# Row sums of the attention: seven tiles added on GpSimd for one pass, and one division for text and image

## The reference, cut to what matters

```python
img_x = attention(q, k_img, v_img)
txt_x = attention(q, k, v, kv_mask)      # kv_mask: only the first context_lens[b] text keys
out = (txt_x + img_x).reshape(b, -1, DIM)
```

## Time and profile before

| | us |
|---|---|
| median of three runs | 3730.16 (3720.81 to 3733.33) |
| the profiled execution | 3734.04 |
| its span on the core | 3731.9 |
| `attend` in the profile, first scores to last exp | about 910 to 2758 |

### The profile page before, as it was taken

One profiled execution on the slowest core, in us unless ns is written; L12 is line 12 of the kernel. 1 busy time (PEld: TensorE's weight loads), 2 busy tenths in 40 slices (PEclk: granted clock), 3 DMA queues, 4 the chain that ended last, 5 costly groups with the idle time before them and its releaser, 6 DMA issues. The chain is left out here.

```text
span 3731.9 us, 54675 instructions
## 1 busy us (share of the span) xinstructions
PE 3280.9 (88%) x18048; PEld 1744.2 (47%) x18048; DVE 2313.9 (62%) x3780; ACT 1483.5 (40%) x2101; POOL 15.6 (0%) x34
## 2 busy tenths in 40 slices
PE   6999999994999999999999999999966631899993
PEld 5788787772333333333333333333224421777772
DVE  5666676654566667667666676676626659333335
ACT  3344444331555555555555555555431110122222
POOL 0000000000000000000000000000000000000000
PEclk8999999995999999999999999999887775999996
DMA  5666666678253453543534535435214550201005
GB/s 153 169 165 165 165 166 166 166 137 151 58 120 78 101 111 69 119 98 81 119 82 97 116 69 113 101 78 119 49 34 158 164 205 3 71 23 45 25 21 180
DMA packets 405977, 402.04 MB, mean 108 GB/s; under 512 B 43569, under 2 KB 326257, under 8 KB 403321
## 3 DMA queue, kind: packets, MB, share of 16 engines
q1 hardware_dynamic: 363272, 367.44, 41.8%
q10 hardware_dynamic: 42624, 33.56, 2.7%
HBM read 262.98 MB, written 137.92 MB: 107 GB/s over the span
## 5 line engine op out<-in xcount | busy, mean ns | idle before, releaser
L834 ACT ACTIVATE at_probs<-at_st 128x1024 f32<-128x1024 f32 (+1 forms) x832 | 852.0, 1024 | 866.1 <-PE at_st L713 860.6
L862 DVE TENSOR_REDUCE at_cm<-at_mx 128x2 f32<-128x896 f32 x768 | 822.0, 1089 | 450.0 <-PE at_mx L729 450.0
L713 PE MATMUL at_st<-at_qst,at_kst 101*128 101x512 f32 (+1 forms) x1664 | 612.2, 449 | 19.2 <-ACT at_probs L834 18.8
L713 PEld LDWEIGHTS at_st<-at_qst,at_kst 101*128 101x128 f32 (+1 forms) x1664 | 243.7, 186 | 731.0 <-ACT at_probs L834 655.4
L752 PE MATMUL at_acc<-at_probs,at_vt 128*32 128x512 f32 (+2 forms) x3584 | 480.1, 610 | 21.8 <-ACT at_ev L815 21.6
L764 PE MATMUL at_acc<-at_probs,at_ones 128*32 128x512 f32 (+2 forms) x3584 | 479.8, 610 | 0.0
L729 PE MATMUL at_mx<-at_kmx,at_qmx 33*128 33x448 f32 (+1 forms) x2048 | 380.1, 423 | 43.5 <-DMA at_kmx<-stack_rows 33.5
L729 PEld LDWEIGHTS at_mx<-at_kmx,at_qmx 33*128 33x128 f32 x2048 | 170.5, 189 | 296.1 <-issue 240.9
L862 DVE TENSOR_REDUCE at_top<-at_mx 128x2 f32<-128x514 f32 x256 | 176.8, 691 | 122.2 <-PE at_mx L729 117.1
L1274 ACT ACTIVATE ff_h<-ff_psa,ff_b1c,alpha 128x512 f32<-128x512 f32 x128 | 99.6, 779 | 378.1 <-PE ff_psa L1256 378.1
L879 DVE RECIPROCAL at_rl<-at_ev 128x512 f32<-128x512 f32 x64 | 210.1, 3324 | 49.4 <-ACT at_ev L815 49.4
(11 more groups left out here) (182 smaller groups left out, 4027.7 us busy)
## 6 DMA issues: line engine op xcount, KB each, us to landing
at_kst<-k_high SPq DMA_DIRECT2D x256, 200.1 KB
at_kmx<-k_high SPq DMA_DIRECT2D x64, 400.2 KB
at_kst<-k_low SPq DMA_DIRECT2D x128, 200.1 KB
pj_xin<-in_ctx_dram SPq DMA_DIRECT2D x96, 256.0 KB, 4.2
k_high<-pj_kh SPq DMA_DIRECT2D x96, 256.0 KB, 3.2
k_low<-pj_kl SPq DMA_DIRECT2D x96, 256.0 KB, 4.7
values<-pj_vs SPq DMA_DIRECT2D x96, 256.0 KB, 4.6
at_vt<-values SPq DMA_DIRECT2D x32, 768.0 KB
```

Source lines behind the costliest of these rows:

```text
L713: pe.matmul(st[0:kn, h % 2, :], kst[p][:, h, t * P:t * P + kn], qst[p][:, h, :], start=True, stop=True).then_inc(S["st_done"], 1)
L834: act.activation(probs[0:kn, SLOT[t], 2 * run:2 * run + 2, :], st[0:kn, :, :], ACT.Exp, scale=SCALE).then_inc(S["exp_done"], 2)
L862: dve.tensor_reduce(dst, mx[:, 2 * slot:2 * slot + 2, 0:kn], AX.X, ALU.max).then_inc(S["mx_free"], 1)
```

## The change

- Sums: the text tiles 0, 1, 2, 4, 5, 7 and 8 have no sums pass of their own. GpSimd adds their probabilities (128x2048 f32 each) in six additions into a new tile `added`, and one pass over `added` stands for all seven. It runs at (12, 1). The passes left are 8 (`SUMMED`): tiles 3, 6, 9 and the text half of 10 at (4, 1), (7, 1), (10, 1), (11, 1); `added` at (12, 1); and the three image passes, all at (0, 1) of the next group.
- Division: GpSimd's `join` forms VT·SI, VI·ST, ST·SI and the sum of the first two (four operations of 128x512); VectorE's `finish` is one reciprocal of ST·SI, one operation that brings in the bias, and one product.
- Waits: a slot of `probs` that held one of the seven tiles is free when its values pass and its addition are done (two waits in `ring` for one). ScalarE copies ST behind (12, 1) and no longer behind (12, 0). The copy of VT waits for `join` in place of `finish`.

```diff
+    SUMMED = [(3, 0, P), (6, 0, P), (9, 0, P), (10, 0, HALF), (None, 0, P), (11, 0, P), (10, HALF, P), (12, 0, KLAST)]
+    NSUM, SUM_IMG0 = len(SUMMED), 5
+    SUMS_AT = {4: [0], 7: [1], 10: [2], 11: [3], 12: [4]}
+    ADDED = [1, 2, 4, 5, 7, 8]
+    NADD = len(ADDED)
@@ GpSimd
+            def join(G, p):
+                pool.wait_ge(S["v_free"], 2 * G + 2)
+                pool.wait_ge(S["s_free"], 2 * G + 2)
+                if not known(G, 1):
+                    pool.wait_ge(S["res_done"], G)
+                pool.tensor_tensor(part[:, 0, :], ev[p][:, VT, :], ev[p][:, SI, :], ALU.mult).then_inc(S["joined"], 1)
+                pool.tensor_tensor(part[:, 1, :], ev[p][:, VI, :], ev[p][:, ST, :], ALU.mult).then_inc(S["joined"], 1)
+                pool.tensor_tensor(rl[:, 0, :], ev[p][:, ST, :], ev[p][:, SI, :], ALU.mult).then_inc(S["joined"], 1)
+                pool.wait_ge(S["joined"], 4 * G + 2)
+                pool.tensor_tensor(rl[:, 1, :], part[:, 0, :], part[:, 1, :], ALU.add).then_inc(S["joined"], 1)
+
+            def add(G, n):
+                t = ADDED[n]
+                pool.wait_ge(S["exp_done"], NST * G + HG * (t + 1))
+                if n:
+                    pool.wait_ge(S["add_done"], NADD * G + n)
+                elif not known(G, 1):
+                    pool.wait_ge(S["s_done"], NSUM * (G - 1) + SUM_IMG0)
+                so_far = added[:] if n else probs[:, SLOT[0]]
+                pool.tensor_tensor(added[:], so_far, probs[:, SLOT[t]], ALU.add).then_inc(S["add_done"], 1)
+
+            def body(i, par):
+                G = 2 * i + par
+                if not known(G, 1):
+                    join(G - 1, 1 - par)
+                for n in range(NADD):
+                    add(G, n)
@@ TensorE, sums and body
+                if t is None:
+                    pe.wait_ge(S["add_done"], NADD * (G + 1))
                 for h in range(HG):
                     cols = slice(h * HD, (h + 1) * HD)
-                    done = pe.matmul(acc[cols, 1, :], ones[r0:r1, :], probs[r0:r1, SLOT[t], h, :],
-                                     start=q in (0, IMG0), stop=q in (IMG0 - 1, NPASS - 1))
+                    src = added[:, h, :] if t is None else probs[r0:r1, SLOT[t], h, :]
+                    done = pe.matmul(acc[cols, 1, :], ones[r0:r1, :], src,
+                                     start=q in (0, SUM_IMG0), stop=q in (SUM_IMG0 - 1, NSUM - 1))
...
-                            for q in (12, 13):
-                                if run == 0:
+                            if run == 0:
+                                for q in (12, 13):
                                     values(G - 1, *before, q)
-                                else:
+                            else:
+                                for q in range(SUM_IMG0, NSUM):
                                     sums(G - 1, q)
                         elif t > 0 and run == 0:
                             values(G, i, par, t - 1)
                         elif t > 0:
-                            sums(G, t - 1)
+                            for q in SUMS_AT.get(t, []):
+                                sums(G, q)
@@ ScalarE, ring and body
+                if u == 0 or u in ADDED:
+                    act.wait_ge(S["v_done"], NPASS * G + u + 1)
+                    act.wait_ge(S["add_done"], NADD * G + max(ADDED.index(max(u, 1)), 0) + 1)
+                else:
+                    act.wait_ge(S["s_done"], NSUM * G + max(q for q in range(NSUM) if SUMMED[q][0] == u) + 1)
...
-                        if (t, run) == (12, 0):
-                            evacuate(G, par, ST, 1, "s_done", "s_free")
+                        if (t, run) == (12, 1):
+                            evacuate(G, par, ST)
@@ VectorE, finish
-                for k, s in enumerate((ST, SI)):
-                    dve.reciprocal(rl[:, k, :], ev[p][:, s, :]).then_inc(S["fin"], 1)
-                for k, v in enumerate((VT, VI)):
-                    dve.wait_ge(S["fin"], 4 * G + k + 1)
-                    dve.tensor_tensor(part[:, k, :], ev[p][:, v, :], rl[:, k, :], ALU.mult).then_inc(S["fin"], 1)
-                dve.wait_ge(S["fin"], 4 * G + 4)
+                dve.wait_ge(S["joined"], 4 * G + 4)
+                dve.reciprocal(part[:, 1, :], rl[:, 0, :]).then_inc(S["fin"], 1)
+                dve.scalar_tensor_tensor(part[:, 0, :], rl[:, 0, :], bv[:, bass.ds(G, 1)], rl[:, 1, :], ALU.mult, ALU.add).then_inc(S["fin"], 1)
+                dve.wait_ge(S["fin"], 2 * G + 2)
                 if not known(G, 2):
                     dve.wait_ge(saved[p], 16 * i)
-                dve.scalar_tensor_tensor(res[p][:], part[:, 0, :], bv[:, bass.ds(G, 1)], part[:, 1, :], ALU.add, ALU.add).then_inc(S["res_done"], 1)
+                dve.tensor_tensor(res[p][:], part[:, 0, :], part[:, 1, :], ALU.mult).then_inc(S["res_done"], 1)
```

More of the change, by code:

```diff
@@ L570, in attend @@
     IMG0 = 11
+    SUMMED = [(3, 0, P), (6, 0, P), (9, 0, P), (10, 0, HALF), (None, 0, P), (11, 0, P), (10, HALF, P), (12, 0, KLAST)]
[3 more added lines that the diff above has]
+    NADD = len(ADDED)
     RING = 4
     SLOT = [3, 0, 1, 2, 0, 1, 2, 0, 1, 2, 0, 1, 2]
-    LAST_PASS = [max(q for q in range(NPASS) if PASS[q][0] == t) for t in range(KT)]
     VT, ST, VI, SI = range(4)
@@ L582, in attend @@
         probs = a.sb("probs", [P, RING, HG, SQ])
+        added = a.sb("added", [P, HG, SQ])
         ones = a.sb("ones", [P, HD])
@@ L600, in attend @@
         names = ("const_set bv_set st_done exp_done v_done s_done mx_full mx_free neg_step top_full top_copied "
-                 "v_free s_free fin res_done const_dve").split()
+                 "v_free s_free add_done joined fin res_done const_dve").split()
         S = {n: a.sem(n) for n in names}
@@ L699, in _ @@
                 pool.memset(where.bitcast(F32), value).then_inc(S["const_set"], 1)
+            def join(G, p):
[23 more added lines that the diff above has]
+                    add(G, n)
+            pairs(pool, body)
+            join(GROUPS - 1, 1)
         @block.tensor
@@ L756, in sums @@
             def sums(G, q):
-                t, r0, r1 = PASS[q]
+                t, r0, r1 = SUMMED[q]
                 if q == 0 and not known(G, 1):
                     pe.wait_ge(S["s_free"], 2 * G)
-                if q == IMG0:
+                if q == SUM_IMG0:
                     pe.wait_ge(S["s_free"], 2 * G + 1)
+                if t is None:
+                    pe.wait_ge(S["add_done"], NADD * (G + 1))
                 for h in range(HG):
                     cols = slice(h * HD, (h + 1) * HD)
-                    done = pe.matmul(acc[cols, 1, :], ones[r0:r1, :], probs[r0:r1, SLOT[t], h, :],
-                                     start=q in (0, IMG0), stop=q in (IMG0 - 1, NPASS - 1))
+                    src = added[:, h, :] if t is None else probs[r0:r1, SLOT[t], h, :]
+                    done = pe.matmul(acc[cols, 1, :], ones[r0:r1, :], src,
+                                     start=q in (0, SUM_IMG0), stop=q in (SUM_IMG0 - 1, NSUM - 1))
                 done.then_inc(S["s_done"], 1)
@@ L809, in copy_top, with evacuate @@
                                ACT.Copy).then_inc(S["top_copied"], 1)
-            def evacuate(G, p, kind, bank, done, free):
-                act.wait_ge(S[done], NPASS * G + (IMG0 if kind < VI else NPASS))
+            def evacuate(G, p, kind):
+                if kind in (VT, VI):
+                    act.wait_ge(S["v_done"], NPASS * G + (IMG0 if kind == VT else NPASS))
+                else:
+                    act.wait_ge(S["s_done"], NSUM * G + (SUM_IMG0 if kind == ST else NSUM))
                 if kind == VT and not known(G, 2):
-                    act.wait_ge(S["res_done"], G - 1)
+                    act.wait_ge(S["joined"], 4 * (G - 1))
+                bank, free = (0, "v_free") if kind in (VT, VI) else (1, "s_free")
                 act.activation(ev[p][:, kind, :], acc[:, bank, :], ACT.Copy).then_inc(S[free], 1)
             def ring(G, t):
[L818 to L823, removed]
+                if t < 4:
+                    if known(G, 1):
+                        return
+                    G = G - 1
+                u = max(u for u in range(t if t >= 4 else KT) if SLOT[u] == SLOT[t])
+                if u == 0 or u in ADDED:
+                    act.wait_ge(S["v_done"], NPASS * G + u + 1)
+                    act.wait_ge(S["add_done"], NADD * G + max(ADDED.index(max(u, 1)), 0) + 1)
+                else:
+                    act.wait_ge(S["s_done"], NSUM * G + max(q for q in range(NSUM) if SUMMED[q][0] == u) + 1)
             def body(i, par):
@@ L838, in body @@
                             if (t, run) == (0, 1):
-                                evacuate(G - 1, 1 - par, VI, 0, "v_done", "v_free")
+                                evacuate(G - 1, 1 - par, VI)
                             if (t, run) == (1, 0):
-                                evacuate(G - 1, 1 - par, SI, 1, "s_done", "s_free")
```

(11 more changed lines are left out.)

2 lines of the change are left out of this document (removed).

## The result

The changed kernel takes 3950.48 us (median of four runs, 3930.48 to 3954.05). The kernel before takes 3731.74 beside it (3720.81 to 3733.98). The ratio is 1.058, with a 95% interval of 1.054 to 1.062. The profiled execution of after is 3954.05, its span 3951.9: 220.0 more than the 3731.9 of before.

What follows compares the result with a forecast made beforehand. TensorE bounds the kernel, with the scores-exp loop of 1.90 us right under it. Nearly balanced groups, gains in groups 0 and 30 and a longer end sum to −2.6 us: 3728 us, eight in ten within 3714 to 3775.

Steps and rivals of the forecast that it cites:

- The loop of 1.90: In `attend`, scores, exp and hand-over make 0.82 + 1.02 + 0.06 = 1.90 us, which no work taken from TensorE can shorten.
- The third pass at (0, 1): The image pass moved to step (0, 1), bound by TensorE, was to cost its full 1.0 us a group.
- The wait at (11, 0): One more ScalarE wait in `ring`, counted only at (11, 0), where TensorE waits for ScalarE's copy: 0.07 us.
- The group: A group of `attend`, 57.27 us before, was to change by −1.04 + 1.00 + 0.07 = +0.03 us at full clock.
- VectorE's `finish`: Division cut to one reciprocal, one product and one addition, nobody waiting soon: 0, except in the last group.
- an addition: GpSimd's sum of two 128x2048 tiles was put at 4.8 us, just in time for the exps: forecast 0.
- rival A: GpSimd late: additions over 4.8 us delay the exp; 3773 at 5.3 us, 3850 at 6.1; chance 0.18 with mild B.
- B: GpSimd and VectorE block each other: up to +1700 us; mild forms share 0.18, strong form shares 0.03 with new stalls.
- The end of `attend`: After the last group, one more pass, then `join`, one reciprocal and one product: +1.4 us.
- rival C: TensorE's idle time lowers its clock: +500 us (4230) if every group drops, +10 to +20 for single drops; chance 0.08.
- Groups 0 and 30: Groups partly at half clock: −3.7 us for group 0, −2.2 for group 30 if its 1.82 us gap comes again.
- D: The 1.82 us gap behind ScalarE's first-run code goes, 3718, or comes twice, 3738; it cost about 10 us; chance 0.11.

## Why the prediction was wrong, point by point

**What held.** The loop of 1.90, named the second bound: at full clock an empty step lasts 1.90 in after and in the four experiments that have any. The third pass at (0, 1): 3.05 became 4.05, its full 1.0. The wait at (11, 0): the forecast 0.07 shows as 2.42 for 2.37 at (12, 0), 0.05. The group: 57.33 where the clock holds, forecast 57.30. VectorE's `finish`: three operations, nobody late.

GpSimd: an addition takes 4.55 us, forecast 4.8; the estimate from the Trainium skill (GPSIMD Engine Reference, Performance versus the Vector engine), 4497 ns, is within 1.3% of the measured 4554. The operations of `join` take 1.27, as forecast. Here is the group that the prediction followed, in a group with the clock at 1.00 up to these steps; (1, 0) starts at 1501.7:

```profile
1504.27 1.27 POOL L711 TENSOR_TENSOR at_part<-at_ev 128x512 f32<-128x512 f32 x1 [26.90 <-ACT at_ev L861]
...
1509.20 4.56 POOL L725 TENSOR_TENSOR at_added<-at_probs 128x2048 f32<-128x2048 f32 x1
...
1513.84 13.85 POOL L725 TENSOR_TENSOR at_added<-at_added,at_probs 128x2048 f32<-128x2048 f32 x3
...
1515.04 1.02 ACT L884 ACTIVATE at_probs<-at_st 128x1024 f32<-128x1024 f32 x1 [1.03 <-PE at_st L749]
```

`join` starts 2.5 behind (1, 0) (forecast 2.7), addition 0 is done at 1513.8, and the exp of (4, 0) at 1515.04, 13.3 behind (1, 0) as forecast, had waited for TensorE's scores and not for `added`. So rival A didn't come. B neither: reductions and additions ran side by side. The rule of the Trainium skill on a port shared as a lock (SBUF — State Buffer, "SBUF: two separate sides") left the reductions out, and the window with 720 us of additions agrees. In this group `finish` begins at 1542.58, 2.6 us behind the last addition.

The end of `attend`: `join`, reciprocal, bias, product.

```profile
2980.99 1.26 POOL L711 TENSOR_TENSOR at_part<-at_ev 128x512 f32<-128x512 f32 x1 [16.19 <-issue]
...
2984.65 1.26 POOL L715 TENSOR_TENSOR at_rl<-at_part 128x512 f32<-128x512 f32 x1
...
2985.94 3.35 DVE L927 RECIPROCAL at_part<-at_rl 128x512 f32<-128x512 f32 x1 [44.10 <-POOL at_rl L715]
...
2989.90 0.69 DVE L932 TENSOR_TENSOR at_res<-at_part 128x512 f32<-128x512 f32 x1
```

The stretch grew by 2.3, forecast 1.4. The terms that the sum has were right to 0.2, but it leaves one out: `finish` also has the operation that brings in the bias, 0.65 us, between the reciprocal and the product.

**The step that failed** is the weighing of rival C, the clock. The sum has a group at +0.03 us "but for the clock below"; in the loop it came to +6.4 us a group (177.9 in 28), nearly all of it steps at the half clock. The prediction said itself that "the other 0.8 us of each pass becomes idle time of TensorE", that the clock had fallen behind a gap of 1.82 and not in the last group with 0.18 idle a step, and "My gaps lie between". Then it gave C 0.08, with the argument that TensorE is at work 80% of the time. Neither ground holds. The known points bracketed the new gap and said nothing on its side; between ends so far apart 0.08 was no reading but a wish. And the busy share is a mean: in the experiment with one pass out only one step of 26 had less work on TensorE than before, and the clock fell in every ninth group.

The last group shows both sizes of rest. In before nearly every one of its steps has a rest of 0.16 to 0.18, and it kept the clock. In after its seven empty steps have no maxima either, so TensorE rests for 1.17 us in them, and the clock fell twice: scores take 1.22 in (2, 1) and (3, 0), and again in (6, 1) to (7, 1). Here are (2, 0), behind the first such rest, and (2, 1):

```profile
2928.21 0.73 PE L749 MATMUL at_st<-at_qst,at_kst 101*128 101x512 f32 x2 [1.17 <-ACT at_probs L884]
2928.88 1.52 PE L788 MATMUL at_acc<-at_probs,at_vt 128*32 128x512 f32 x8
2930.33 1.22 PE L749 MATMUL at_st<-at_qst,at_kst 101*128 101x512 f32 x2
```

The group took 55.3 for 48.9, 5.4 more than forecast. In before and in the four experiments without an empty step the last group has no step at the half clock. So the row of 0.18 was read rightly; it said nothing on rests four to seven times as long.

**The price of C** was worked out for a fall in every group that lasts until tile 10: "2.3 more than now together" for a tile, 16 us a group and +500 in all. Its steps were right: 3.90 to 4.06 in run 0 (forecast 3.9) and 2.40 when empty (forecast 2.42). The longest falls of the loop, from (4, 0) to (10, 1), cost 17.2 us. What was too large is how often and how long: of the 22 groups that fell, six did so behind (3, 1), six behind (5, 1) and ten only behind (8, 1) or (9, 1), and six had no fall. That gives 178 us in 28 groups, and 220 in all. The prediction had nothing between "One or two single drops" (+10 to +20) and +500.

**Small terms.** The sum says groups 1 to 30 and counts 29, which is right, as group 30 has a term of its own. Groups 0 and 30 were forecast at −3.7 and −2.2 and gave −1.9 and +16.1. Group 0 had one more fall, behind (9, 1), which cost it about 1.4. Group 30 began with a stall in its first step, which lasted 6.79, where before had its stall of 1.82 in tile 8:

```profile
2838.03 1.02 ACT L884 ACTIVATE at_probs<-at_st 128x1024 f32<-128x1024 f32 x1 [5.22 <-issue]
...
2839.20 1.19 PE L749 MATMUL at_st<-at_qst,at_kst 101*128 101x512 f32 x2 [3.50 <-ACT at_probs L884]
```

The next step, 7.38, is the one with three passes, now at the half clock, and the clock stayed down through (8, 1) and fell once more behind (9, 1). That is what D's "As well it may come twice" was about, but D had put 10 us on it, and the group came out 18 over its forecast.

**What stays open.** Why the clock comes back when it does. In group 10 of after it fell in (4, 0) and was back in (6, 0); in group 8 it fell in (4, 0) and was back only in (11, 0). In the loop of after it was never later than that, and (10, 1) is the first step without maxima. The runs show no rule for it. Nor do they show why the same rest of 0.78 takes the clock in one group and not in the next.

## What to carry to other kernels

Before taking work from an engine that is busy 98% look at what it will do in that time: if the answer is "wait", nothing is won, and on TensorE the rest itself can cost the clock of the steps behind it, up to 46 us of them here. Where a second bound stands right under the first, take away only as much as lets the work be dealt out evenly again, one pass to a step here, and take it from the steps that are longer than the rest. And when the new case lies between two measured ones, one harmless and one not, give the bad side a real chance and the forecast a width to match.

## What the runs showed of the hardware that I had not expected

- One rest of 0.78 us in a group of 57 us was enough to lose TensorE's clock, in every ninth group, and did nothing in the others; three in a row cost it in 25 groups of 28, three apart in 9, and seven (three, two and two in a row) in 22 with the change as it is and in all 28 without its GpSimd work and its third pass. The Trainium skill (TensorE: Matmul & The Clock Gate, "A second HAM failure mode: psum-queue depth-cycling") tells of a kernel in which TensorE idles briefly but often between groups of matmuls and the clock goes up and down. The traces here agree with it, and show that one rest in 57 us can be enough.
- Once at half clock, TensorE was busy 96% (11.50 of 12.00 us, window above) and stayed there; in group 8 of after the steps at it, (4, 0) to (10, 1), add up to 46 us.
- Matmuls with zero weights held the clock of the loop as well as useful ones: it is 1.00 for both fillings of the seven steps.
- GpSimd's addition of two f32 tiles is 4554 ns for 128x2048, 2401 for 128x1024 and 1269 for 128x512 (a product, the last), that is 2.2 to 2.5 ns an element, with VectorE reducing beside it.
